# GNN message passing: two float32r table pieces and more dense groups in the 128-wide one-hot passes

## The reference

```
agg = segment_sum(h[src] * norm, dst)              # L0: two GCN layers, 64 wide inside
agg = segment_sum(x[src], dst)                     # L1: one mean layer, 128 wide
m = relu(h[src] + edge_attr)                       # L2: five GIN layers, 128 wide
agg = segment_sum(m, dst)
alpha = (q[dst] * (k[src] + e)).sum(-1)            # L3: two attention layers, 4 heads
```

## Time and profile before

| | us |
|---|---|
| median of 3 runs | 12353.79 (12352.64 to 12357.77) |
| the profiled execution | 12353.87 |
| its span, first to last instruction | 12352.0 |
| the two 64-wide passes | 319 to 2211 |
| the 128-wide "sum" pass | 2301 to 3262 |
| the five 128-wide "edge" passes | 3364 to 8788, about 1000 each |
| the two attention layers | from about 8960 on |

### The profile page before, as it was taken

The page is one execution under the profiler, slowest core; times in us unless marked ns, Lnnn a source line. Parts: engine busy times, 40 slices in busy tenths (PEclk is TensorE's granted clock), DMA queues, the critical chain, the costliest instruction groups (busy, mean ns, idle before and its releaser), DMA issues. The chain is left out here.

```text
span 12352.0 us, 299461 instructions
## 1 busy us (share of the span) xinstructions
PE 8931.0 (72%) x56600; PEld 6630.0 (54%) x56601; DVE 8070.8 (65%) x22450; ACT 5168.7 (42%) x13292; POOL 8044.8 (65%) x8530
## 2 busy tenths in 40 slices
PE   2788688688678868886886888688756646566645
PEld 1677577466455645654554555455444435444444
DVE  6677687555567766775675677667744458644478
ACT  3554454444455555555555555555411111111110
POOL 0777677577477747756774776577367757477755
PEclk9899799799889979998997999799855559655577
DMA  1211111222244434424443443344245544355533
GB/s 43 39 31 29 37 31 31 55 55 55 54 112 111 111 85 111 110 80 115 111 111 85 111 111 91 106 110 111 62 139 153 154 114 137 104 152 152 153 106 100
DMA packets 1310096, 1163.44 MB, mean 94 GB/s; under 512 B 238842, under 2 KB 1105822, under 8 KB 1308784
## 3 DMA queue, kind: packets, MB, share of 16 engines
q0 software_dynamic: 272544, 566.00, 18.3%
q1 hardware_dynamic: 1036880, 591.36, 16.8%
HBM read 1007.40 MB, written 149.12 MB: 94 GB/s over the span
## 5 line engine op out<-in xcount | busy, mean ns | idle before, releaser
L969 POOL DMA_INDIRECT rings<-rows_key,idx x4536 | 4356.3, 960 | 2161.1 <-issue 1312.8
L1153 DVE TENSOR_TENSOR bigDE<-bigDE,part 128x128 f32 (+1 forms) x6656 | 1891.4, 284 | 1394.1 <-PE part L1064 413.5
L1064 PE MATMUL part<-rings 128*128 128x128 f32 (+1 forms) x11920 | 1714.7, 290 | 747.6 <-ACT rings L1005 426.2
L632 POOL DMA_INDIRECT bigDE<-rows_key_value,idx x1664 | 1636.4, 983 | 852.2 <-issue 470.1
L1077 PE MATMUL wide<-bigDE,bigC 128*128 128x384 bf16 x10800 | 1956.0, 338 | 246.1 <-DVE bigC L1135 225.6
L1064 PEld LDWEIGHTS part<-rings 128*128 128x128 f32 (+1 forms) x11920 | 1561.4, 190 | 922.4 <-issue 786.0
L996 ACT ACTIVATE rings<-iota,relK 128x128 f32<-128x128 f32 x5960 | 1900.3, 389 | 4.9 <-issue 1.5
L969 POOL DMA_INDIRECT rings<-rows_hidden,idx x1424 | 1386.5, 974 | 676.8 <-issue 409.2
L1077 PEld LDWEIGHTS wide<-bigDE,bigC 128*128 128x128 bf16 x10800 | 1072.0, 101 | 989.8 <-issue 400.3
L1135 DVE TENSOR_SCALAR bigC<-bigC,node 128x512 bf16<-128x512 int16 x4410 | 1388.7, 380 | 45.7 <-issue 44.0
L988 ACT COPY idx<-srcK 128x4 int32 (+1 forms) x1490 | 283.6, 191 | 2469.0 <-PE part L1064 2308.2
(11 more groups left out here) (272 smaller groups left out, 10280.3 us busy)
## 6 DMA issues: line engine op xcount, KB each, us to landing
rings<-in_attr SPq DMA_DIRECT2D x3780, 64.0 KB
walk_value<-bigDE SPq DMA_DIRECT2D x416, 256.0 KB, 3.1
rings<-walk_value SPq DMA_DIRECT2D x416, 256.0 KB
rings<-rows_key,idx POOLq DMA_INDIRECT x4536
bigDE<-rows_key_value,idx POOLq DMA_INDIRECT x1664
bigF<-in_attr SPq DMA_DIRECT2D x380, 64.0 KB
rings<-rows_hidden,idx POOLq DMA_INDIRECT x1424
rows_key<-rings SPq DMA_DIRECT2D x60, 320.0 KB, 3.0
```

Source lines behind the costliest of these rows:

```text
L632: e.indirect_dma_start(gbuf[:, g, r, 0:table.shape[1]], None, table, bass.IndirectOffsetOnAxis(ap=c.idx[:, g, r:r + 1], axis=0)).then_inc( ...
L969: e.indirect_dma_start(to[:, r, 0:width], None, table, bass.IndirectOffsetOnAxis(ap=idx[:, r:r + 1], axis=0)).then_inc(gate.sem, 16)
L1064: last = e.matmul(part[0:width, bank(n), r, :], msg[:, r, 0:width], sel[:, r, :], start=True, stop=True)
L1153: e.tensor_tensor(into, into, got, ALU.add).then_inc(c.added.sem, 1)
```

## The change

`_mixed` gets its sizes from the room: `per`, `cuts` (the number of pieces), `depth` (the ring of one-hots) and `turn`. The 64-wide passes keep theirs (6, 3, 14). In the 128-wide passes the table is cut into two float32r pieces: the upper one has the low 12 bits masked off, the lower one is the rest. The one-hots are float32r too (2 KB for each partition instead of 1 KB), in a ring of 8 instead of 14. `high` falls away, `first` becomes a mask with one source on DVE, `merge` has two operations instead of three. `per` goes from 10 to 6 in the "sum" pass (14 turns of 14 groups, 28 dense groups instead of 18, a lead of 12) and from 10 to 8 in the "edge" passes (11 turns of 18 groups, 22 dense groups instead of 18, a lead of 10). The code of `_pass` for kinds that are no longer used goes, and three waits of its "attend" kind no longer count a tick.

```diff
-def _room(c, spare):
+def _room(c, over, per):
     r = Ctx()
-    r.depth = 14
-    first, second = c.E[:, 0:30 * 192].bitcast(BF16), c.F[:, 0:19 * 192].bitcast(BF16)
+    r.per, r.cuts, r.depth, r.turn = per, 2, 8, 52
+    spare = {"bigB": c.Bwide, "bigC": c.C}[over]
+    upper, lower = c.rounded_pieces
+    ring = c.rounded_hots[over]
...
-    r.hots = [spare[:, k * 256:(k + 1) * 256].bitcast(BF16) for k in range(14)]
+    r.hots = [ring[:, k * GROUP * P:(k + 1) * GROUP * P] for k in range(r.depth)]
...
-    per, skip, rounds = (10, 12, 9) if width == D else (6, 2, 14)
+    per, cuts, turn = room.per, room.cuts, room.turn
     body = 2 * per
     items = body + 2
-    lead = items - skip
+    rounds, lead = divmod(GROUPS - STEPS, items)
+    lead += STEPS
+    skip = items - lead
...
                 for r in range(GROUP):
-                    last = e.matmul(wide[:, r, 0:3 * width], hot[:, r * P:r * P + P],
+                    last = e.matmul(wide[:, r, 0:cuts * width], hot[:, r * P:r * P + P],
...
-                    e.tensor_tensor(to, third(2), room.attr, ALU.add).then_inc(c.summed.sem, 1)
+                    e.tensor_tensor(to, part_of(cuts - 1), room.attr, ALU.add).then_inc(c.summed.sem, 1)
...
-                _hold(e, c.summed, done * 2 + 1, c.tick_dve)
-                e.tensor_tensor(to, to, third(1), ALU.add).then_inc(c.summed.sem, 1)
-                _hold(e, c.summed, done * 2 + 2, c.tick_dve)
-                e.tensor_tensor(to, to, third(0), ALU.add).then_inc((c.joined if edge else c.message).sem, 1)
+                if cuts == 3:
+                    _hold(e, c.summed, done * 2 + 1, c.tick_dve)
+                    e.tensor_tensor(to, to, part_of(1), ALU.add).then_inc(c.summed.sem, 1)
+                _hold(e, c.summed, (done + 1) * (cuts - 1), c.tick_dve)
+                e.tensor_tensor(to, to, part_of(0), ALU.add).then_inc((c.joined if edge else c.message).sem, 1)
...
-                _hold(e, c.spent, i * (2 * NODE_TILES) + (half * NODE_TILES + s + 1 - depth), c.tick_dve)
-                e.tensor_scalar(hots[(half * NODE_TILES + s) % depth], room.sources[half], c.node[:, s:s + 1], None,
+                _hold(e, c.spent, i * (2 * NODE_TILES) + freed(half, s), c.tick_dve)
+                e.tensor_scalar(hots[slot(half, s)], room.sources[half], c.node[:, s:s + 1], None,
                                 ALU.is_equal).then_inc(c.hot.sem, 1)
...
+                    e.tensor_scalar(upper(t).bitcast(I32), staged(t).bitcast(I32), UPPER, None, ALU.bitwise_and
+                                    ).then_inc(c.rest.sem, 1)
...
-                    elif kind == "attend":
-
-                        _hold(e, c.expanded, q + 1, c.tick_pe)
-                        _hold(e, c.keyed, q + 1, c.tick_pe)
-                        _hold(e, c.scored, q + 1, c.tick_pe)
+                    e.wait_ge(c.expanded.sem, c.expanded.at(q + 1))
+                    e.wait_ge(c.keyed.sem, c.keyed.at(q + 1))
+                    e.wait_ge(c.scored.sem, c.scored.at(q + 1))
...
-        room = _room(c, B)
+        room = _room(c, "bigB", 6)
...
-        room = _room(c, C)
+        room = _room(c, "bigC", 8)
```

More of the change, by code:

```diff
@@ L650, in _ @@
                         index(q + 2, (g + 2) % RING, i + (g + 2) // RING)
[L651 to L658, removed]
+                        _hold(e, c.product, q - 1, c.tick_act)
+                        e.wait_ge(c.turned.sem, c.turned.at(q + 1))
+                        e.activation(turn[:, g % 2, :, :], turned[:, g % 2, :, :], ACT.Copy
+                                     ).then_inc(c.message.sem, 1)
         @block.tensor
@@ L681, in _ @@
                     _hold(e, c.added, (q - banks + 1) * GROUP, c.tick_pe)
[L682 to L685, removed]
[L686 to L697 removed]
+                    e.wait_ge(c.expanded.sem, c.expanded.at(q + 1))
+                    e.wait_ge(c.keyed.sem, c.keyed.at(q + 1))
+                    e.wait_ge(c.scored.sem, c.scored.at(q + 1))
+                    for r in range(GROUP):
+                        last = e.matmul(part[:, b, r, 0:cell], c.sel[:, g, r, :], msg[:, g, r, :],
+                                        start=True, stop=True)
                     last.then_inc(c.product.sem, 1)
@@ L703, in prepare @@
                 scores = None if score is None else score[:, bass.ds(q * GROUP * HEADS, GROUP * HEADS)]
[L704 to L709, removed]
+                if kind == "look":
                     b = g % 2
@@ L865, in _mixed @@
     assert total * GROUP >= EDGE_TILES + NODE_TILES - 1 and (total + 2) * GROUP <= KCOLS
-    assert body % RING == 0 and body * NODE_TILES // per % depth == 0 and lead >= STEPS
+    assert body % RING == 0 and 2 * turn % depth == 0 and STEPS <= lead < items
     def place(n):
@@ L915, in staged, with upper, slot, freed @@
         return room.stage[t % 2][:, 0:count * width].rearrange("p (t f) -> p t f", f=width)
+    def upper(t):
+        count = min(TURN, NODE_TILES - t * TURN)
+        return room.upper[t % 2][:, 0:count * width].rearrange("p (t f) -> p t f", f=width)
+    def slot(half, s):
+        return (half * turn + s) % depth
+    def freed(half, s):
+        spins, at = divmod(half * turn + s - depth, 2 * turn)
+        half, s = divmod(at, turn)
+        return spins * 2 * NODE_TILES + half * NODE_TILES + min(s + 1, NODE_TILES)
     with ExitStack() as ctx:
@@ L1206, in _mixed @@
         c.row[b].passed(16 * (STEPS // 2))
-    for g in (c.high, c.rest, c.middle, c.low):
+    for g in (c.rest, c.middle, c.low):
         g.passed(STEPS)
+    if cuts == 3:
+        c.high.passed(STEPS)
 def _chunk(i, size=CHUNK):
```

93 lines of the change are left out of this document (44 added, 49 removed).

## The result

The changed kernel takes 12841.5 us (median of 4 runs, 12832.5 to 12848.5) and the kernel before 12355.8 (12352.6 to 12361.9): a ratio of 1.0392, 95% interval 1.0374 to 1.0410. The change costs 3.9%, 486 us; 2.7%, 333 us, was forecast. The profiled execution took 12844.3 us, 490 more than that of before.

What follows compares the result with a forecast made beforehand. POOL's gathers set every turn before; after the change DVE was to set the sum and edge turns. 12353.9 + 98 (sum pass) + 235 (five edge passes) = 12687, say 12690 us, 2.7% more; range 12200 to 12940.

Steps and rivals of the forecast that it cites:

- The hots: One-hot writes on DVE in 128-wide passes: 480 ns each, 133 ns more; 13.0 us more a turn, plus 1.2 for delays.
- The gathers at 1.25 us: POOL's gathers in the changed passes stay at 1.25 us each: 60.0 us a sum turn, 80.0 us an edge turn.
- DVE sets the edge turn at 88.5: Edge passes: DVE needs 88.5 us a turn against POOL's 80.0, so each pass takes 47 us more, five +235.
- DVE sets the sum turn at 70.7: Sum pass: DVE needs 70.7 us a turn against POOL's 60.0, so the pass takes 98 us more.
- PE at 62 us: TensorE's matmuls and scatters take 62 us of a sum turn and 67 of an edge turn, under DVE.
- The attention waits: Three plainer waits in the "attend" passes: no cost or gain counted; 40 us if that were wrong.
- The signs named: Profile signs expected: 480 ns hots, 71 and 88 us turns, POOL waiting for indices, PE for hots, DVE not for rows.
- POOL keeps the turns: Rival, chance 0.12: hots cost DVE little more, POOL's gathers still set the 128-wide turns, total 12204 us.

Runs made afterwards that it cites:

- the thin hots: The changed kernel with DVE writing the 128-wide passes' one-hots as bfloat16 and matmuls taking the table's pieces as fixed operand: 12378.5 us, 1.0007 of the kernel before.

## Why the prediction was right, and where not

The range held the time, and the sign was right; the loss of 486 us is half as much again as the 333 that were forecast. That the turns came out within 2 us of the forecast was luck: neither is set by the engine that was said to set it. Step by step:

- *The hots.* Right for a single one: 483 ns for 480, and undelayed hots start 0.396 us apart where it was 0.263, 133 ns more. That they would be delayed more (1.2 us a turn) was wrong in sign: they are delayed less than before, 4 ns on average instead of 33, and the delay went to the gathers. On average within a run of hots they start 0.402 us apart, 0.297 before, so they cost DVE 98 x 0.105 = 10.3 us more a turn, and not 14.2.
- *The gathers at 1.25 us.* This is the step that failed. I kept POOL's need in an edge turn at 64 x 1.25 = 80.0 us. The wide write of the hots made it 64 x 1.405, 89.9 us, shown by the thin hots, and POOL set the turn once more.
- *DVE sets the edge turn at 88.5.* Wrong in its owner, and close in its number by luck. DVE needs 82.5, as the run with fewer gathers shows; 3.9 of the 6 us too much lie in the hots. For POOL the 80.0 was 9.9 us too little. Which of the two was the larger need was therefore wrong as well: 82.5 against 89.9, where I had 88.5 against 80.0. From first hot to first hot the turn is 90.4 us, and it was 102.1 before, near the 102.6 which I took from one stretch. That makes 11 x 1.9 + 9 x 0.5 = 25 us more a pass than forecast, nearly the whole way from 47 to 73.
- *DVE sets the sum turn at 70.7.* The number was met (71.2, the pass +97 for +98), the owner was not. Neither DVE nor POOL sets it: taking 10 us of work from DVE, or a quarter of its gathers from POOL, left it in place. What is left is PE's work and the hand-over at the end of each dense group. That lifting PE's work shortens the turn was not shown, as the run meant for it fell in one of the sessions in which everything was slower; that adding to PE's work lengthens it was.
- *PE at 62 us.* Right in the sum pass (523.5 us busy of 600 are 62.1 a turn), 3 us too little in the edge pass (470.1 are 69.9, for 67), and float32r streams once: 28 and 16 expands of an edge turn took 3.58 and 2.15 us, so 0.119 each for the 0.111 forecast. But a free TensorE of 9 us in the turn isn't slack if it is all in one dependency: the first hots of a dense group wait for the merge of the one before.
- *The attention waits.* Costed at nothing, since DVE waited for PE only 6.6 us, with a gain of 40 us (0.1 us in each of 416 groups) if that reasoning were wrong. They lost 38 us. That the size is that of the bound is chance: the sign is the other one, and a loss was not among what I had weighed.
- *The signs named.* Hots of 480 ns, turns of 71 and 88, PE waiting for hots, expand at about 0.11: seen. POOL's idle time put down to indices, and DVE no longer waiting for rows: not seen, and they were the ones which told the owner.

Of the rivals, *POOL keeps the turns* had its mechanism for the edge pass, with the opposite sign: POOL did keep the turn, and the change lost by it. The Trainium skill has the ground for this in "SBUF — State Buffer", section "Who interferes with whom": VectorE in its 2-port modes, the fastest ones, and GpSimd need the same pair of SBUF ports, and whoever comes second is blocked. I read the modes only as a price for DVE and left out what they take from POOL. The runs agree that the two hold each other up: gathers have a mean of 957 ns in passes with 2-byte hots and 1106 with 4-byte ones. That with 2-byte hots it is the hots that give way, and with 4-byte hots the gathers, they show too, but not why.

No version tried beats the kernel before in an ordinary session: its 102.1 us edge turns with 80 gathers cost 1.28 us a gather, where the changed kernel pays 1.41.

## What to carry to other kernels

When an operand becomes wider, price what the wider write does to the engine that moves data beside it, and not only to the engine that writes: here 0.13 us more on DVE were hidden, and 0.10 us more on POOL were not. A turn's length that comes out as predicted doesn't show which engine set it; take away work from each engine in turn and look at which removal moves it. Price a denser schedule by what it saves (here 5% and 2% of the gathers) against what it repeats (11 or 14 dense rounds instead of 9), before asking whether a cheaper type makes room for it.

## What the runs showed of the hardware

- A DVE operation that writes 512 float32r elements delays a concurrent indirect DMA on GpSimd (mean 957 to 1106 ns over a pass, 1.8 us for one that begins in the last hot before a two-source operation) and is hardly delayed itself (483 ns mean over 479); one that writes bfloat16 is delayed (380 ns mean over 345) where a gather ends in it, and leaves the gather nearly alone (0.96 us over 0.944).
- A two-source float32 DVE operation of 512 elements (`join`) delays a gather that begins within it as well, in both kernels: means of 1.08 us before and 1.17 after.
- Float32r matmuls of 256 columns stream at 0.12 us each with their 4-byte weight loads beside them, one record for each.
- In some sessions the turns of every `_mixed` pass are 6 to 29 us longer, between instructions, while single instructions and the attention passes nearly keep their times (the first one 396.6 us with the old waits there, and 400.3 in the ordinary session). The same chip was seen in both conditions. What is behind it stays open, and there the order of two kernels can turn round.
